# Decoder layer on one core: norms of the last pass in another order, Wo loaded one block per batch, high parts on VectorE with a sum, and one head of eight multiplied unsplit

## The reference

```python
x = layernorm(x + gated(x, w_gate, w_up, w_down))        # silu, smallest half zeroed, * up, down
q, k, v = x @ Wq, ctx @ Wk, ctx @ Wv                     # 32 heads of 32, 8 kv heads
p = softmax(q @ k.T * 32 ** -0.5)                        # per head, 112 x 375
x = layernorm(x + (p @ v) @ Wo)
y = x.astype(bf16) @ w3.T.astype(bf16)                   # w3 from 4-bit weights
x = layernorm(x + y)
```

## Time and profile before

| what | value |
|---|---|
| median of 3 runs | 2794.39 us (2790.82 to 2797.74) |
| the profiled execution, its own time | 2799.27 us |
| its span, first to last instruction | 2797.5 us |
| PE busy | 2484.3 us (89%) |
| POOL busy | 1310.1 us (47%) |
| DVE busy | 1264.6 us (45%) |
| ACT busy | 1026.5 us (37%) |
| mean granted clock of TensorE | 0.939 |
| attend pass, first load to last reciprocal | about 1978 to 2476 us of the span |
| finish pass | about 2478 to 2797.5 us |

### The profile page before, as it was taken

One profiled execution on the slowest core, in us unless ns is written; L12 is line 12 of the kernel. 1 busy time (PEld: TensorE's weight loads), 2 busy tenths in 40 slices (PEclk: granted clock), 3 DMA queues, 4 the chain that ended last, 5 costly groups with the idle time before them and its releaser, 6 DMA issues. The chain is left out here.

```text
span 2797.5 us, 32188 instructions
## 1 busy us (share of the span) xinstructions
PE 2484.3 (89%) x12640; PEld 2133.6 (76%) x12640; DVE 1264.6 (45%) x1574; ACT 1026.5 (37%) x1507; POOL 1310.1 (47%) x595
## 2 busy tenths in 40 slices
PE   7999699999999999999999997599669899968886
PEld 7999699888998889988899886589446666536564
DVE  4852007830068300683006830643348888724543
ACT  2112236332363323633236331211147677721111
POOL 5433345845458454583545832300257667631110
PEclk9999899999999999999999998699679999979998
DMA  5554422324223232232422323664546666564451
GB/s 195 179 187 156 158 99 105 106 95 135 98 98 113 95 129 103 100 110 93 137 102 98 113 81 128 177 193 116 143 123 167 166 159 163 136 153 121 129 134 38
DMA packets 228521, 359.10 MB, mean 128 GB/s; under 512 B 107184, under 2 KB 163504, under 8 KB 227664
## 3 DMA queue, kind: packets, MB, share of 16 engines
q1 hardware_dynamic: 228368, 357.02, 42.1%
HBM read 277.57 MB, written 78.70 MB: 127 GB/s over the span
## 5 line engine op out<-in xcount | busy, mean ns | idle before, releaser
L689 POOL TENSOR_TENSOR gp_w_lo<-gp_raw,gp_w_hi 128x1024 fp32r<-128x1024 f32 (+2 forms) x268 | 642.2, 2398 | 605.3 <-ACT gp_w_hi L596 604.9
L58 PE MATMUL gp_acc<-gp_x_hi,gp_w_hi 128*128 128x448 f32 x1376 | 512.7, 373 | 25.5 <-POOL gp_w_lo L689 19.2
L59 PE MATMUL gp_acc<-gp_x_lo,gp_w_hi 128*128 128x448 f32 x1376 | 504.4, 367 | 0.0
L60 PE MATMUL gp_acc<-gp_x_hi,gp_w_lo 128*128 128x448 f32 x1376 | 503.7, 366 | 0.0
L1237 POOL TENSOR_TENSOR ap_e_lo<-ap_e,ap_e_hi 125x1344 fp32r<-125x1344 f32 x96 | 294.0, 3069 | 147.3 <-ACT ap_e_hi L1265 72.0
L596 ACT CAST gp_w_hi<-gp_raw 128x1024 fp32r<-128x1024 f32 (+2 forms) x268 | 273.2, 1022 | 215.3 <-PE gp_acc L60 156.3
L58 PEld LDWEIGHTS gp_acc<-gp_x_hi,gp_w_hi 128*128 128x128 f32 x1376 | 259.8, 189 | 47.3 <-issue 19.4
L58 PE MATMUL gp_acc<-gp_h_hi,gp_w_hi 128*128 128x448 f32 (+1 forms) x704 | 272.9, 388 | 21.2 <-POOL gp_w_lo L689 15.9
L1304 DVE TENSOR_REDUCE ap_n_max<-ap_p_s 112x2 f32<-112x750 f32 x256 | 236.7, 938 | 95.5 <-PE ap_p_s L1359 94.3
L334 DVE TENSOR_REDUCE gp_sel_unit<-gp_keys 112x4 f32<-112x2048 f32 x4 | 9.1, 2286 | 591.1 <-ACT gp_keys L609 591.1
L60 PEld LDWEIGHTS gp_acc<-gp_x_hi,gp_w_lo 128*128 128x128 f32 x1376 | 259.7, 189 | 20.8
(11 more groups left out here) (153 smaller groups left out, 4626.1 us busy)
## 6 DMA issues: line engine op xcount, KB each, us to landing
gp_raw<-in_w_gu SPq DMA_DIRECT2D x172, 512.0 KB, 3.2
gp_raw<-in_w_d SPq DMA_DIRECT2D x80, 512.0 KB, 3.3
cp_c_raw<-in_ctx_t SPq DMA_DIRECT2D x32, 750.0 KB, 6.6
q_scratch<-qp_q_out SPq DMA_DIRECT2D x64, 224.0 KB, 2.6
ap_qs<-q_scratch SPq DMA_DIRECT2D x32, 448.0 KB, 5.9
o_scratch<-ap_o_ab SPq DMA_DIRECT2D x64, 224.0 KB
ap_vs<-v_scratch SPq DMA_DIRECT2D x16, 773.4 KB
k_scratch<-cp_k_out SPq DMA_DIRECT2D x16, 752.0 KB
```

The costliest lines, as they stand in the source:

```text
L58: nc.tensor.matmul(out, wh, xh, start=first, stop=False)
L59: nc.tensor.matmul(out, wh, xl, start=False, stop=False)
L60: return nc.tensor.matmul(out, wl, xh, start=False, stop=last)
L689: last = nc.gpsimd.tensor_tensor(o, i, hi.bitcast(F32), ALU.subtract)
```

## The change

Four edits: (1) in the finish pass DVE does `norm(i + 1)` before `last(i)`, and POOL's roots and the counts that DVE waits for follow; (2) in the attend pass Wo's block n is loaded in batch n at head 2 and split at head 6 (step 20 on ACT), for batches 0 to 7, and nothing of it stands before batch 0; (3) DVE's high part becomes a `tensor_scalar` (times 1.0) that also writes a sum nobody uses; (4) `FULL` is (3,) in place of (3, 7), so head 7 is split: its high part on DVE (at step 0 of the next batch, after pair 2's maximum), its low part on POOL, six fp32r matmuls on PE.

```diff
-    FULL = (3, 7)
+    FULL = (3,)
     HI_ACT = (1, 2, 4)
     HI_DVE = tuple(h for h in range(KV) if h not in HI_ACT + FULL)
     LO_POOL = tuple(h for h in range(KV) if h not in FULL)
-    W_FIRST = 2
+    W_LOAD_AT, W_SPLIT_AT = 2, 6
+        e_sum = m.sb("e_sum", [KN, 1], F32)
 # SP
-            for k in range(W_FIRST):
-                load_w(k)
-                    if n == 0 and W_FIRST + h < KV:
-                        load_w(W_FIRST + h)
+                    if h == W_LOAD_AT and n < KV:
+                        load_w(n)
 # POOL
-            for k in range(W_FIRST):
-                split_w(k)
-                if W_FIRST <= g < KV:
-                    split_w(g)
+                if g % KV == W_SPLIT_AT and g // KV < KV:
+                    pool.wait_ge(lo_pool, upto(LO_POOL, g - 1))
+                    split_w(g // KV)
 # ACT
-                    if t == 2 and n == 0 and W_FIRST + h < KV:
-                        split_w(W_FIRST + h)
+                    if x == KT * W_SPLIT_AT + 2 and n < KV:
+                        split_w(n)
 # DVE, split_hi
-                nc.vector.tensor_copy(e_hi[g % NHI][:], e[g % NE][:]).then_inc(hi_dve, 1)
+                if g > HI_DVE[0]:
+                    dve.wait_ge(hi_dve, upto(HI_DVE, g) - 1)
+                nc.vector.tensor_scalar(e_hi[g % NHI][:], e[g % NE][:], 1.0, None, ALU.mult, ALU.add,
+                                        accum_out=e_sum[:]).then_inc(hi_dve, 1)
 # finish, POOL
+            root(0)
             for i in range(NTILE):
-                root(2 * i)
                 if i + 2 < NTILE:
                     split_lo(i + 2)
                 root(2 * i + 1)
+                if i + 1 < NTILE:
+                    root(2 * i + 2)
 # finish, DVE
+            norm(0)
             for i in range(NTILE):
-                norm(i)
                 if i + 2 < NTILE:
                     quotients(i + 2)
+                if i + 1 < NTILE:
+                    norm(i + 1)
                 last(i)
```

More of the change, by code:

```diff
@@ L1238, in _ @@
                                             ALU.subtract).then_inc(lo_pool, 1)
-                    if g < KV:
-                        pool.wait_ge(lo_pool, upto(LO_POOL, g))
         @block.scalar
@@ L1568, in norm @@
                 layer_norm(nc, dve, own[:], stats, mv, var_eps, rstd, own[:], ready, rooted,
-                           2 * i + 1).then_inc(y2_done, 1)
+                           max(2 * i, 1)).then_inc(y2_done, 1)
             def last(i):
@@ L1578, in last @@
                 layer_norm(nc, dve, own[:], stats, mv, var_eps, rstd, own[:], ready, rooted,
-                           2 * i + 2).then_inc(fin_done, 1)
+                           min(2 * i + 3, 2 * NTILE)).then_inc(fin_done, 1)
             quotients(0)
             quotients(1)
+            norm(0)
             for i in range(NTILE):
-                norm(i)
                 if i + 2 < NTILE:
                     quotients(i + 2)
+                if i + 1 < NTILE:
+                    norm(i + 1)
                 last(i)
```

## The result

The changed kernel took 2680.15 us (median of 4 runs, 2678.68 to 2687.68) beside 2792.61 us for the kernel before (4 runs, 2787.49 to 2797.74): a ratio of **0.9603, 95% interval 0.9577 to 0.9629**. The forecast was 2683, in a range of 2658 to 2718. The profiled execution took 2678.68 us, 120.6 less than the profiled one of before; the sum had said 111.2. The medians of the two kernels lie 112.5 apart.

The account below looks back on a forecast made before the run. PE was taken as held by Wo loads at the attend pass's start, T to step 9, and norm queued behind last; -73.8 - 41 + 6.3 - 2.7 = -111.2 from 2799.3, less 4.9 to the median: 2683 us, range 2658 to 2718.

Parts of the forecast that it names:

- Norm order: Finish pass: PE's wait before the turn goes, the tile period falls from some 20.5 to 15.1 us; -73.8 us.
- Wo by batch: Start of the attend pass: the first two periods lose their Wo waits, 49 us against 90; -41 us, bounds -45 and -30.
- The sum and head 7: Attend pass: DVE slower between T and step 9, ten ordinary periods +6.3 us; three periods with an inversion -2.7 us.
- DVE keeps up: Attend pass: DVE's pitch is shorter or PE's slack hides it, 13 periods lose 1.0 us each; near 2666, chance 0.13.
- the sum changes nothing: Attend pass: DVE's high part still takes two ports and waits for POOL; 16 us more, 2699, chance 0.06.
- the slower case: Attend pass: each of four high parts takes POOL's whole 3.07 us on top; 2795 and more, chance 0.04.
- loads bind: Finish pass: issue and landing of loads take over 14 us, period nearer 17.5; 29 us more, 2712, chance 0.14.
- half the start: Start of the attend pass gives half, from half clock and late q and k; +20 us, 2703, chance 0.09.

## Why the prediction was right

**Norm order, forecast -73.8.** Measured -74.5 in the two profiles: linear(0) to linear(12) takes 183.4 us where it took 246.1 (-62.7; forecast -64.8, a period of 15.1 for 15.28), and from there to the end -11.8 (forecast -9.0). The forecast period was 0.2 too short, mostly because the working took 0.2 us for a slow first matmul off linear and did not put it on the product that follows: linear takes 3.28 us, the 48 matmuls 11.2, not 10.9. Not all of the 5.3 us that a tile gained is the wait: 3.4 are, and most of the rest is the turn and the 18 matmuls behind it, which took 6.7 us at the clock of before and take 5.0 now. In the tail linear(12) to the last turn takes 4.84 in place of 13.86, the -9.0 forecast; the rest of the end, which was to stay, takes 14.3 in place of 17.1, and the granted clock of the last 20 us is 0.89 where it was 0.67. The loads did not bind. Alone, the edit gave 2.7%, which is 76 us of 2806: the step stands by itself.

**Wo by batch, forecast -41.** Measured -42.0, with 23.35 us for the first period (forecast 23) and 24.71 for the second (26). Within the first there is an error that cost nothing: the first scores came 3.7 us after the turn, not 5.3, because ACT took up nm_hi 0.4 us after it. The 19 steps behind them took 19.6 us, not 17.7, and took it back; the mean clock from 2001 to 2025 us is 0.73, after 0.50 in the 16 us before. Alone: 1.43%, 40 us, and its profile has 41.8 less in the two periods.

**The sum and head 7, forecast +6.3 and -2.7.** The mechanism is right by its own rows: high parts of 1.55 + 0.08 (forecast 1.61), step 9 at T + 11.37 (11.45), a wait before pair 7 of 1.01 (1.3), and head 7's high part given to ACT takes that wait away. By the Trainium skill (SBUF - State Buffer, section Who interferes with whom) the form that writes out its accumulator stays out of the two-port mode; the trace agrees, with 1540 to 1555 ns beside a working POOL, against 843 to 3704 for the copy. The tier table of the Trainium skill's VectorE: DVE Perf Modes gives fp32 `tensor_scalar` twice the rate, without that exception; the copy alone takes 0.85 us here, the form with the sum 1.55, so for this form the trace does not agree.

The sizes were off. Ten ordinary periods cost +9.2: seven of them average 25.83 (forecast 25.97), and three, of 27.0 to 27.6, hold something that the forecast did not have. Windows of the changed kernel around such a wait for k:

```profile
2158.00:2160.00 2.00, 0.36 (x2) 0.00 (x0) 0.80 (x2) 1.18 (x3) 1.92 (x2) 1.00 0.49 147
2160.00:2162.00 2.00, 1.99 (x7) 1.69 (x8) 0.94 (x1) 0.54 (x1) 1.92 (x2) 0.67 0.55 125
2162.00:2164.00 2.00, 2.00 (x7) 1.61 (x7) 0.95 (x2) 0.54 (x1) 2.00 (x1) 0.50 1.01 250
2164.00:2166.00 2.00, 2.00 (x11) 1.60 (x10) 2.00 (x2) 1.50 (x3) 0.94 (x1) 0.98 1.02 224
```

PE stood 1.66 us for k until 2160.01, and in the 4 us after it the granted clock was 0.67 and then 0.50, the lower level of 1.2 GHz: 7 matmuls in 2 us where it is 11 at 0.98. The three inversions gave -8.8 (forecast -2.7, bound -8). One of them, DVE in the kernel after:

```profile
2127.57 1.55 DVE L1312 TENSOR_SCALAR_CACHE_REDUCE ap_e_hi<-ap_e 125x1344 fp32r<-125x1344 f32 x1 [0.77 <-ACT ap_e L1254]
...
2129.05 0.85 DVE L1318 RECIPROCAL ap_den<-ap_den 128x112 f32<-128x112 f32 x1
2129.81 0.20 DVE L1302 SCALAR_TENSOR_TENSOR ap_nm_lo<-ap_p_s,ap_nm_hi 32x112 fp32r<-32x112 f32 x1
```

Here nm_lo starts 1.86 us after the turn; before it was 2.82, behind a copy of 2.52. Step 0 waits 0.79 us for it in place of 1.41, and the clock stays at 1.00 where it had gone to 0.50.

The part between T and step 9 is settled, by several profiles (median of the ordinary periods at full clock):

| kernel | T to step 9, us | ordinary periods with a fall of the clock, of ten |
|---|---|---|
| before | 10.82 | 0 |
| norm order alone | 10.73 | 5 |
| high part with a sum alone | 10.85 | 5 |
| changed | 11.38 | 3 |
| changed, second profile | 11.38 | 7 |
| changed, two heads unsplit | 10.84 | 5 |
| changed, head 7's high part on ACT, two profiles | 10.28, 10.31 | 7, 6 |

So head 7's split with its high part on DVE costs 0.5 to 0.6 us a batch (forecast 0.63), 5 to 6 us in ten. The rest of both terms is not settled.

The kernel with the norm order alone has the attend pass of before, unchanged, and in its profile two of three inversion periods are 27.5 and 26.4 us and five ordinary ones 26.8 to 27.2, with waits for k of 1.5 to 2.1 us where they were mostly 1.3 to 1.6; its one inversion period without a fall took 26.43, no more than the changed kernel's, so most of the -8.8 is the clock. And a second profile of the changed kernel took 8.8 us more from first to last turn than the first (399.4 for 390.6). What varies is k's landing and whether the clock falls, and the stop does not decide that by its length alone: in this second profile one of 1.98 us had no fall behind it and one of 1.55 had. What decides it no run shows.

The timed runs say what can be said: edits 1 and 2 alone add up to 4.1%, and the whole change gave 4.0 and 4.4% on two chips, so edits 3 and 4 together are about nothing, as the forecast had them (+3.6 us).

The rest is small: from the last turn to linear(0) it was -2.4 (forecast 0, 3 either way) and in the passes before -2.2, and -74.5 - 42.0 + 9.2 - 8.8 - 2.4 - 2.2 is -120.7, beside 120.6 measured.

That 2683 lies within 3 us of 2680.15 is partly luck. The sum missed the difference of the profiles by 9.4 us, mostly by the inversion periods, the last batch and the passes before; the profiled run of before was the slowest of its kernel and that of the changed kernel the fastest, and the medians lie only 112.5 apart. What the forecast can claim is edits 1 and 2, 114.8 us in it and 116.5 in the profiles.

Of the rivals, *DVE keeps up* is ruled out by the wait before pair 7, *the sum changes nothing* and the slower case by high parts of 1.55 us, *loads bind* by the period of 15.28, and *half the start* by 23.35.

## What to carry to other kernels

When an instruction queues behind one that waits for another engine, count both orders: swapping `norm` and `last` gave about 75 us without taking away any work. A wait of about 1.5 us on PE is priced by what the clock does after it as well: in this kernel a fall costs an ordinary period about 1.5 us. Before a load is moved forward, look at what else is in flight and who waits for it: here the wait went to other rows, among them the sums that only every fourth batch needs. Where a gain is off by a few us in one profile, look at a second profile of the same kernel before explaining it, and compare a stretch that the varying wait does not touch, such as T to step 9 at full clock.

## What the runs showed of the hardware that I had not expected

- After a stop of 1.66 us the granted clock fell to 0.50; after stops of 1.41 and 1.59 us for the same load it did not, and in another profile of the same kernel it fell after 1.55 and not after 1.98. The ordinary periods of the changed kernel's first profile therefore come in two lengths, near 25.8 and near 27.4.
- Issued 2.5 us earlier, the last block of k landed 1.2 us later (12.2 us in flight in place of 8.5); issued ahead of v as well, it landed after 6.0 us, and other loads came late.
- DVE's plain copy next to POOL spans 843 to 3704 ns; the form with a sum stays within 15 ns (1540 to 1555), and the read of the sum adds 82 ns.
